# Moving steps in the hand-written order of a two-batch recurrence: second factors, outputs and weight loads

## The chip, the cores and the metric

The kernel runs on one core of a Trainium2 chip. The metric is device time in microseconds (us), median of the runs. TensorE is PE in the profile, VectorE is DVE, ScalarE is ACT, GpSimd is POOL, and SyncE (SP) only issues DMAs here.

## The reference, cut to what matters

Two layers work on x of 2 batches x 1024 tokens x 256 channels. The change touches only the first one's attention, a linear recurrence with a decay for each channel and token (4 heads of 64). Its core:

```
def step(S, inputs):
    rt, kt, vt, wt = inputs
    kv = kt[..., :, None] * vt[..., None, :]
    y = jnp.einsum('bhi,bhij->bhj', rt, S + u[None, :, :, None] * kv)
    S = wt[..., :, None] * S + kv
    return (S, y)
...
yn = ((y - mean) * jax.lax.rsqrt(var + LN_EPS)).reshape(b, t, c)
yn = yn * ln_w + ln_b
return yn @ W_o
```

Ahead of it r, k, v and w come from matrix products of the mixed input (x and its shift by one token). Behind it follow an expert stage, a sparse attention, a local attention and a feed-forward stage, all untouched by the change.

## The kernel before

`phase_b` computes the recurrence without a loop over tokens. The 1024 tokens of a batch are 8 blocks of 128. Within a block the token pairs are covered by a diagonal step and seven **levels** (h = 1, 2, 4 ... 64), each for both halves c of the channels. The steps, as they are named in the list `ORDER` (name, batch, rest):

- `m`, `x j`, `d1`, `d2`, `k`, `r`, `v`: the projections of a batch. For each `x` step, PE makes four products (L472), DVE takes them out of PSUM (L726) and adds one input (L728), and GpSimd adds three (L836).
- `D c`: the diagonal, PE at L515, DVE at L801. It reads `ru`, the second factor (r times a vector), which GpSimd makes (L842).
- `L h c`: a level. PE multiplies (L534; in batch 1 two large bf16 products of an identity, L521, whose result nobody reads, go ahead of it). Then DVE scales one factor (L738, called rE below) and for h up to 16 copies the result under a mask (L816); GpSimd scales the other factor (L853, called kF). The next level of the same half waits for both rE and kF of this one.
- `W`: block decays, seven halving products on DVE (L748). In batch 1 they write where the mixed inputs lay, so they wait until the `v` products are done.
- `kE`: PE transposes the keys (L456), ACT copies them (L676). `S c`: PE products (L551), then seven dependent state updates on DVE (L757).
- `y g`: the outputs of blocks 4g to 4g+3: PE at L571 and L575, ACT copies (L683). They wait for states of both halves. `stats`, `scale`: normalization on DVE (L768 to L785), with a square root on ACT (L687).
- `yn g`, `o g`: PE transposes (L456), ACT scales (L692), PE multiplies by W_o (L591), DVE adds to x (L826).

Every engine walks the same list and leaves out what is not its own, so the place of a step in `ORDER` sets its place on PE, DVE, ACT, GpSimd alike. `in_turn` merges lists by spreading each evenly over the whole. PSUM banks are taken in a ring of eight in the same order. The last `o` step of the phase lets the expert stage begin (PE at L1070). SyncE loads the next stage's weights (L437 to L444) over batch 0's space, behind a wait.

Of the kernel before, what the change touches and what calls it, by code (L numbers as in the profile page):

```python
# [19 lines left out]
D = 256  # L20
# [92 lines left out]
def kmaj(ap, c=2):  # L113
    return ap.rearrange("(c p) n -> p c n", c=c)
# [20 lines left out]
def adapter(K, tag, k, n_ids, idx0, names, hT, ready, ready_x):  # L135
# [6 lines left out]
    s_xb, s_var, s_std, s_norm = (K.sem(f"{tag}_{n}") for n in ("xb", "var", "std", "norm"))  # L142
    ORDER = [("z", n, b) for b in range(B) for n in range(2)] + [("y", t, 0) for t in range(TB_)] + [("y", t, 1) for t in range(4)]
    ORDER += [("T", c, g, 0) for c in range(2) for g in range(2)] + [("y", t, 1) for t in range(4, TB_)] + [("T", c, g, 1) for c in range(2) for g in range(2)]
    for s in ORDER:
        ring.plan((tag,) + s, "dve" if s[0] == "y" else "act")
# [17 lines left out]
    def pe(e, w):  # L164
        for s in ORDER:
            b, key = s[-1], (tag,) + s
            i = ring.bank(key)
            if s[0] == "z":
                n = s[1]
                w.wait_ge(s_w[b], 64)  # L170
                ready(w, b)
                w.wait_ge(*ring.free(key))
                for c in range(2):
                    h = e.matmul(PS[0:k, i, :], ws[b].wd[:, c, :], hT[b][:, c, 512 * n:512 * n + 512], start=c == 0, stop=c == 1)
            elif s[0] == "y":
                t = s[1]
                w.wait_ge(*ring.emptied((tag, "z", t // 4, b)))
                w.wait_ge(*ring.free(key))
                h = e.matmul(PS[:, i, 0:D], ws[b].zT[0:k, P * t:P * t + P], ws[b].wu[0:k, :], start=True, stop=True)
            else:  # L180
                _, c, g, _ = s
                w.wait_ge(s_norm, 8 * b + 4 * g + 4)
                w.wait_ge(*ring.free(key))
                for j in range(4):
                    h = e.transpose(PS[:, i, P * j:P * j + P], ws[b].y[:, 4 * g + j, P * c:P * c + P], K.ident)
            h.then_inc(ring.sem, 1)
# [114 lines left out]
def in_turn(*lists):  # L301

    at = [((j + 0.5) / len(z), n, s) for n, z in enumerate(lists) for j, s in enumerate(z)]
    return [s for _, _, s in sorted(at)]


def phase_b(K):
# [3 lines left out]
    a, PS, ring, X, cv, arena, ident = K.a, K.PS, K.ring, K.X, K.cv, K.arena, K.ident  # L311
# [18 lines left out]
    A, ru, kE, Wl, St, st = [], [], [], [], [], []  # L330
    for space in (arena.down(9840), shared):
# [3 lines left out]
        o, z = 6144, {}  # L335
# [23 lines left out]
    def project(b):  # L359
        return [("m", b)] + [("x", b, j) for j in range(4)] + [("d1", b), ("d2", b)] + [("W", b)] * (1 - b) + [("k", b), ("r", b), ("v", b)] + [("W", b)] * b  # L360

    def pairs(b):
        return [("D", b, c) for c in range(2)] + [("L", b, h, c) for h in LEVELS for c in range(2)]

    def close(b, late):


        norm = [("stats", b, 0), ("stats", b, 1), ("scale", b, 0), ("scale", b, 1)] if late else [("stats", b, 1), ("scale", b, 1)]
        first = [("y", b, 0)] + [("stats", b, 0)] * (1 - late) + [("y", b, 1)] + [("scale", b, 0)] * (1 - late)
        return [("kE", b), ("S", b, 0), ("S", b, 1)] + first + norm + [(n, b, g) for g in range(2) for n in ("yn", "o")]  # L370

    ORDER = project(0) + [("mx", 1)] + in_turn(pairs(0), project(1)) + in_turn(close(0, 1), pairs(1)) + close(1, 0)

    for s in ORDER:
        b = s[1]
# [29 lines left out]
    s_bx, s_decay, s_ru, s_rE, s_kF, s_W, s_S, s_var, s_sqrt, s_yn = (  # L405
        K.sem("b_" + n) for n in ("xx", "decay", "ru", "re", "kf", "w", "s", "var", "sqrt", "yn"))
# [3 lines left out]
    def n_level(b, h, c):  # L410

        return 14 * b + 2 * LEVELS.index(h) + c + 1

    def n_W(b, h):
        return 7 * b + LEVELS.index(h) + 1
# [8 lines left out]
    def lower(z, h):  # L424
        return z.rearrange("p (m two j) -> p m two j", two=2, j=h)[:, :, 0, :]
# [7 lines left out]
    K.b_done = K.end = b_done  # L433

    def sp(e, w):
        w.wait_ge(*ring.emptied(("o", 0, 3)))
        e.dma_start(K.W1c, kmaj(a["L0_cond2_W1"])).then_inc(s_wc, 16)  # L437
        for b in range(B):
            r = e.value_load(K.ids[0:1, 2 + b:3 + b], min_val=0, max_val=E - 1)
            e.dma_start(K.Wc[b][:, :, 0:192], a["L0_cond2_W2"].rearrange("(f p) n -> p f n", f=8)).then_inc(s_wc, 16)  # L440
            e.dma_start(K.Wc[b][:, :, 192:256], a["L0_cond2_We"].rearrange("e (f p) n -> e p f n", f=8)[bass.ds(r, 1)].rearrange("e p f n -> (e p) f n")).then_inc(s_wc, 16)
            e.dma_start(K.bc[b][:, 0:192], a["L0_cond2_b2"].partition_broadcast(P)).then_inc(s_wc, 16)
            e.dma_start(K.bc[b][:, 192:256], a["L0_cond2_be"][bass.ds(r, 1)].rearrange("e n -> (e n)").partition_broadcast(P)).then_inc(s_wc, 16)
        e.dma_start(K.Wg, kmaj(a["L0_ffn_Wg"])).then_inc(s_wc, 16)  # L444

    def pe(e, w):
# [147 lines left out]
        w.wait_ge(K.s_tmix_w, 128)  # L594
        for name, b, *s in ORDER:
            if name == "m":
# [231 lines left out]
    def pool(e, w, own):  # L828
        for name, b, *s in ORDER:
            if name == "x":  # L830
                j, = s
                n, c = NC[j]
                sl = slice(512 * n, 512 * n + 512)
                for f in (1, 3, 2):
                    w.wait_ge(*ring.emptied(("x", b, j, f)))
                    e.tensor_tensor(xf[f][:, c, sl], xf[f][:, c, sl], K.hT2[b][:, c, sl], ALU.add).then_inc(s_xf[f], 1)  # L836
            elif name == "D":
                c, = s
                if b:
                    w.wait_ge(*ring.filled(("v", 1, 3)))  # L840
                w.wait_ge(*ring.emptied(("r", b, 1, 1)))
                e.tensor_scalar(ru[b][:, c], rT[b][:, c], cv("faaaa", c), 1.0, ALU.mult, ALU.mult).then_inc(s_ru, 1)  # L842
            elif name == "L":
                h, c = s
                if h > 1:
                    w.wait_ge(s_W, n_W(b, h // 2))
                    w.wait_ge(s_kF, n_level(b, h // 2, c))
                else:
                    w.wait_ge(s_decay, 4 * b + 4)
                low = lower(kT[b][:, c], h)  # L850
                Wh = Wl[b][h][:, c].rearrange("p (m two) -> p m two", two=2)
                w.wait_ge(*ring.filled(("L", b, h, c, 1)))
                e.tensor_tensor(low, low, Wh[:, :, 1:2].broadcast_to([P, S // (2 * h), h]), ALU.mult).then_inc(s_kF, 1)  # L853

    return sp, pe, act, dve, pool


# [1601 lines left out]
def build(nc, a, out, stop=None):  # L2459
    with ExitStack() as ctx:  # L2460
# [20 lines left out]
        for name, phase in (("x0", phase_b), ("x1", phase_d), ("c2", phase_e), ("x2", phase_f), ("x3", phase_g)):  # L2481
            stages.append(phase(K))
            if stop == name:
                break
# [111 lines left out]
```

## Time and profile before

| | us |
|---|---|
| time, median of 3 runs | 2020.78 (2017.02 to 2028.28) |
| time of the profiled execution | 2041.56 |
| its span | 2039.8 |
| PE busy, share of the span | 1886.8, 93% |
| DVE busy | 1108.7, 54% |
| POOL busy | 459.2, 23% |
| the recurrence's merged part, from `D 0 0` on PE to its last `o` step | 102 to 334 |

The engine shares are for the whole span; the touched phase is 11% of it. There the row of the granted TensorE clock is what to look at beside the waits: it stands at full (1.00, 2.4 GHz) or half (0.50, 1.2 GHz).

### The profile page before, as it was taken

Reading aid. Unit: us, or ns where it says so; the run is one execution under the profiler, and the core shown is the slowest. Engines: PE = TensorE matmul, PEld = TensorE weight load, DVE = VectorE, ACT = ScalarE, POOL = GpSimd, SP = SyncE. Lnnn points to the kernel's source line nnn. Section 1 sums busy time; section 2 is a strip of 40 time slices with the busy share of each in tenths; the row PEclk is TensorE's granted clock in tenths of the full one; section 3 lists DMA queues with packets and bytes.
Section 4 is the critical chain, followed back from the end, with each engine's and each line's share of the span. In section 5 each row is a group of like instructions: output and inputs, shape, how many; then the busy total and the mean of one; then the engine's idle time right before and its main releaser. Section 6 shows DMA issues by size and latency. Waiting matters only on the chain.

```text
span 2039.8 us, 37916 instructions
## 1 busy us (share of the span) xinstructions
PE 1886.8 (93%) x15705; PEld 1378.7 (68%) x15705; DVE 1108.7 (54%) x2301; ACT 944.4 (46%) x1689; POOL 459.2 (23%) x512
## 2 busy tenths in 40 slices
PE   5989998995997978899999999999999999999997
PEld 3466876673664654677777777766777777787776
DVE  4474543017123125788888788854555554445544
ACT  2213022111233304788888888854455544445522
POOL 1353110004121033222121212112223222223212
PEclk8779578996998988999999999999999999999999
DMA  4000021111343347741011211000000000010001
GB/s 131 0 1 2 1 68 43 52 56 56 99 144 114 97 132 191 139 76 38 21 36 37 91 25 33 20 22 1 2 2 1 1 1 2 1 27 2 2 1 42
DMA packets 89309, 92.22 MB, mean 45 GB/s; under 512 B 34914, under 2 KB 74786, under 8 KB 88994
## 3 DMA queue, kind: packets, MB, share of 16 engines
q1 hardware_dynamic: 82882, 78.01, 14.2%
q0 software_dynamic: 3456, 9.44, 1.7%
q8 instruction: 125, 2.05, 0.4%
q10 hardware_dynamic: 2800, 2.34, 0.4%
q14 instruction: 46, 0.38, 0.1%
HBM read 67.23 MB, written 23.07 MB: 44 GB/s over the span
## 4 chain that ended last, share of the span: by engine, by line
PE 79%; ACT 7%; DVE 6%; DMA 3%; issue 2%; POOL 2%; another core or an unknown queue 0%; SPq 0%; POOLq 0%; DVEq 0%
PE PS L1627 9%; PE PS L1086 8%; PE PS L1641 7%; PE PS L1077 7%; PE PS L1952 6%; PE PS L1997 6%; PE PS L2013 5%; PE PS L1987 5%; ACT arena L1721 3%; PE PS L1618 3%; PE PS L534 3%; PE PS L1957 3%; ACT arena L1717 2%; PE PS L480 1%; PE PS L2020 1%
## 5 line engine op out<-in xcount | busy, mean ns | idle before, releaser
L1800 DVE CUSTOM_DVE_ANT_0 arena<-PS,arena 128x1024 f32<-128x1024 f32 x256 | 312.2, 1220 | 68.2 <-PE PS L1618 64.1
L1721 ACT ACTIVATE arena<-arena 128x1024 f32<-128x1024 f32 x256 | 297.4, 1162 | 9.3 <-DVE arena L1800 9.2
L1627 PE MATMUL PS<-arena 128*128 128x128 f32 x2048 | 278.4, 279 | 0.4 <-ACT arena L1717 0.2
L1627 PEld LDWEIGHTS PS<-arena 128*128 128x128 f32 x2048 | 229.2, 142 | 60.2 <-issue 27.1
L2200 POOL TENSOR_SCALAR arena<-arena 128x448 f32<-128x448 f32 (+1 forms) x256 | 153.5, 616 | 393.6 <-DVE arena L2128 392.5
L2099 ACT ACTIVATE arena<-arena 128x449 f32<-128x449 f32 (+1 forms) x256 | 161.5, 633 | 141.3 <-DVE arena L2137 141.3
L1717 ACT COPY arena<-PS 128x512 f32<-128x512 f32 x298 | 171.4, 590 | 78.3 <-PE PS L1627 77.0
L1077 PE MATMUL PS<-arena 128*128 128x512 f32 x384 | 170.2, 601 | 6.6 <-ACT arena L1183 6.6
L1086 PE MATMUL PS<-arena 128*128 128x256 f32 x768 | 172.2, 385 | 0.0
L2137 DVE CUSTOM_DVE_ANT_0 arena<-PS,arena 128x448 f32<-128x448 f32 (+1 forms) x256 | 136.8, 589 | 59.9 <-PE PS L1988 58.8
L1086 PEld LDWEIGHTS PS<-arena 128*128 128x128 f32 x768 | 147.2, 193 | 23.3 <-issue 1.8
L1618 PE MATMUL PS<-arena 96*128 96x512 bf16 x512 | 154.4, 382 | 6.4 <-DVE arena L1800 3.8
L1641 PEld LDWEIGHTS PS<-arena 128*17 128x17 f32 x4096 | 103.6, 97 | 71.3 <-issue 67.7
L1807 DVE COPY arena<-PS 128x512 f32<-128x512 f32 x214 | 147.3, 688 | 6.6 <-PE PS L1627 2.0
L1641 PE MATMUL PS<-arena 128*17 128x128 f32 x4096 | 137.8, 273 | 13.3 <-ACT arena L1730 12.8
L1240 DVE TENSOR_TENSOR arena<-PS,arena 128x512 f32<-128x512 f32 x24 | 16.6, 692 | 234.4 <-PE PS L1086 226.3
L2143 DVE COPY arena<-PS 128x512 f32<-128x512 f32 (+1 forms) x128 | 83.9, 656 | 105.4 <-PE PS L1997 104.6
L1077 PEld LDWEIGHTS PS<-arena 128*128 128x128 f32 x384 | 72.8, 192 | 96.8 <-issue 96.7
L1997 PE MATMUL PS<-arena 128*128 128x128 f32 x960 | 130.3, 277 | 1.8 <-ACT arena L2105 1.8
L1997 PEld LDWEIGHTS PS<-arena 128*128 128x128 f32 x960 | 106.4, 141 | 30.1 <-issue 25.5
L1952 PE MATMUL PS<-arena 128*128 128x512 f32 x256 | 123.2, 605 | 1.8 <-ACT arena L1739 0.8
L2013 PE MATMUL PS<-arena 128*64 128x128 f32 x1920 | 119.8, 275 | 0.0
(294 smaller groups left out, 2728.6 us busy)
## 6 DMA issues: line engine op xcount, KB each, us to landing
arena<-in_L_ffn_W SPq DMA_DIRECT2D x16, 1024.0 KB, 7.2
arena<-prior SPq DMA_DIRECT2D x16, 512.0 KB, 4.0
parts<-arena SPq DMA_DIRECT2D x24, 256.0 KB, 6.4
arena<-parts SPq DMA_DIRECT2D x96, 64.0 KB, 2.9
arena<-parts SPq DMA_DIRECT2D x48, 128.0 KB, 9.6
prior<-arena SPq DMA_DIRECT2D x4, 1024.0 KB
ye<-arena SPq DMA_DIRECT2D x7, 512.0 KB, 3.0
ya<-arena SPq DMA_DIRECT2D x7, 512.0 KB, 5.0
```

Of the source, the lines that this page charges most:

```text
L1077: h = e.matmul(PS[:, i, :], wt[:, k, P * f:P * f + P], src[:, k, s0:s0 + 512], start=k == 0, stop=k == 1)
L1086: h = e.matmul(PS[:, i, D * j:D * j + D], src[:, f, P * (t + j):P * (t + j) + P], wt[:, f, :], start=f == 0, stop=f == 7)
L1618: i = e.matmul(PS[:, SBK[z % 2] + n, :], Q6[m % 2][0:96, h, :], K6[m // TB_][0:96, h, 512 * n:512 * n + 512], start=True, stop=True)
L1627: h = e.transpose(PS[:, i, P * j:P * j + P], Sb[z % 3][:, 512 * g + P * j:512 * g + P * j + P], ident)
L1641: i = e.matmul(PS[32 * d:32 * d + 17, OBK, P * g:P * g + P], V4[b][:, k, h + d, :], Pt[(z + d) % 8][:, P * k:P * k + P], start=k == 0, sto ...
L1717: e.copy(Pt[z % 8][:, 512 * g:512 * g + 512], PS[:, group(key, r), :]).then_inc(r.into(key), 1)
L1721: e.activation(Sb[z % 3], Sb[z % 3], ACT.Exp, bias=mr[:, z % 4:z % 4 + 1], scale=-1.0).then_inc(s_exp, 1)
L1800: e.tensor_tensor_reduce(Sb[z % 3], ps, Ab[m % 2], 1.0, 3e38, ALU.add, ALU.min, mr[:, z % 4:z % 4 + 1]).then_inc(s_ttr, 1)
L1952: h = e.matmul(PS[:, i, :], wt[:, k, fs], x_[:, k, 512 * n:512 * n + 512], start=k == 0, stop=k == 1)
L1997: h = e.transpose(PS[:, 4 + d, P * j:P * j + P], Pb[x % 8][:, P * j:P * j + P], ident)
L2013: h = e.matmul(PS[c, YB, P * (t % 4):P * (t % 4) + P], wt, Pt[(2 * z + d) % 4][:, P * j:P * j + P], start=j == 0, stop=j == nj - 1)
L2099: e.activation(Pb[x % 8][:, 0:wd + 1], sbt[:, 0:wd + 1], ACT.Exp, bias=mr[:, g:g + 1], scale=-1.0, accum_out=sm[:, g:g + 1]).then_inc(s_ex ...
```

## The change

Three steps are moved and one wait is loosened.

1. `ru` of batch 1 is no longer made by GpSimd at the `D` steps but at two entries of their own, placed at the end of batch 1's projections. As that list grows from 12 to 14 entries, `in_turn` also puts every projection step of batch 1, `W 1` among them, a little earlier between the levels of batch 0.
2. Three empty entries (`("wait", 0)`, which every engine passes over) are put into batch 0's closing list, so that `y 0 0` stands behind `L 1 2 1` instead of behind `L 1 1 1`, and what follows is shifted too; `yn 0 1` and `o 0 1` leave that list and go behind `S 1 1`.
3. SyncE's weight loads wait for batch 0's second `scale` instead of its last `o`.

```diff
-    ORDER = project(0) + [("mx", 1)] + in_turn(pairs(0), project(1)) + in_turn(close(0, 1), pairs(1)) + close(1, 0)
+    c0, c1, rest = close(0, 1), close(1, 0), ("wait", 0)
+    c0 = c0[:3] + [rest, rest] + c0[3:4] + [rest] + c0[4:]
+    ORDER = project(0) + [("mx", 1)] + in_turn(pairs(0), project(1) + [("ru", 1, 0), ("ru", 1, 1)]) + in_turn(c0[:-2], pairs(1)) + c1[:3] + c0[-2:] + c1[3:]
...
-        w.wait_ge(*ring.emptied(("o", 0, 3)))
+        w.wait_ge(s_yn, 2)
...
-            elif name == "D":
+            elif name == ("ru" if b else "D"):
```

The program's lines behind it are three further down in the changed kernel. DVE at the end of batch 0's levels, before (the halving products of `W 1` are L748, rE is L738, with 8x64 for level 64 and 16x32 for level 32):

```order
89 L738 TENSOR_TENSOR arena<-arena 128x16x32 x2
90 L738 TENSOR_TENSOR arena<-arena 128x8x64
91 L748 TENSOR_TENSOR arena<-arena 128x1024
...
97 L748 TENSOR_TENSOR arena<-arena 128x16
98 L738 TENSOR_TENSOR arena<-arena 128x8x64
```

And in the changed kernel:

```order
89 L741 TENSOR_TENSOR arena<-arena 128x16x32
90 L751 TENSOR_TENSOR arena<-arena 128x1024
...
96 L751 TENSOR_TENSOR arena<-arena 128x16
97 L741 TENSOR_TENSOR arena<-arena 128x16x32
98 L741 TENSOR_TENSOR arena<-arena 128x8x64 x2
```

`W 1` now stands ahead of rE of `L 0 32 1`, which `L 0 64 1` on PE waits for; before, only rE of `L 0 64 1` stood behind it.

PE from batch 1's values (L504) to the first output (L571), before:

```order
31 L504 MATMUL PS<-arena 128x256 x16
32 L534 MATMUL PS<-arena 128x64 x32
33 L515 MATMUL PS<-arena 128x128 x16
...
43 L534 MATMUL PS<-arena 128x64 x16
44 L521 MATMUL PS<-arena 128x512 x2
45 L571 MATMUL PS<-arena 128x64 x16
```

In the changed kernel (L507 and L574):

```order
31 L507 MATMUL PS<-arena 128x256 x16
32 L537 MATMUL PS<-arena 128x64 x64
33 L518 MATMUL PS<-arena 128x128 x16
...
43 L537 MATMUL PS<-arena 128x64 x16
44 L524 MATMUL PS<-arena 128x512 x2
45 L537 MATMUL PS<-arena 128x64 x16
46 L524 MATMUL PS<-arena 128x512 x2
47 L537 MATMUL PS<-arena 128x64 x16
48 L524 MATMUL PS<-arena 128x512 x2
49 L574 MATMUL PS<-arena 128x64 x16
```

Four levels of batch 0 instead of two stand between the values and the diagonal, and two levels of batch 1 are put ahead of the first output.

## Rows read from the trace of the kernel before

**Rows 1.** Stretches of the phase: busy us of each engine, granted clock, DMA.
```profile
core 0: us, PE busy (x) PEld busy (x) DVE busy (x) ACT busy (x) POOL busy (x), PEclk, DMA share, GB/s
118.00:145.30 27.30, 24.23 (x151) 16.97 (x152) 26.26 (x31) 0.59 (x1) 22.08 (x15) 0.50 0.00 1
...
189.60:193.10 3.50, 3.50 (x33) 3.28 (x32) 3.36 (x8) 0.00 (x0) 1.01 (x1) 0.51 0.00 0
193.10:206.70 13.60, 12.18 (x179) 9.85 (x179) 11.52 (x25) 2.05 (x4) 3.00 (x2) 1.00 0.00 1
206.70:275.00 68.30, 68.30 (x447) 57.85 (x446) 38.06 (x85) 5.59 (x12) 11.83 (x9) 0.50 0.00 1
275.00:298.90 23.90, 20.38 (x229) 16.88 (x229) 8.35 (x24) 7.09 (x14) 4.67 (x3) 1.00 0.51 143
298.90:326.20 27.30, 23.10 (x122) 20.97 (x122) 11.94 (x53) 3.92 (x8) 0.00 (x0) 0.50 0.01 2
```
**Rows 2.** PE, timeline: start, us, instructions, idle before them and its releaser.
```profile
182.09 3.79 PE L534 MATMUL PS<-arena 64*128 64x64 f32 x64
189.41 3.60 PE L515 MATMUL PS<-arena 64*128 64x128 f32 x32 [3.53 <-POOL arena L842]
192.94 2.00 PE L456 MATMUL PS<-arena 128*128 128x128 f32 x16
...
206.41 6.78 PE L571 MATMUL PS<-arena 128*128 128x64 f32 x32 [1.43 <-DVE arena L757]
213.12 2.83 PE L575 MATMUL PS<-arena 64*128 64x64 f32 x24
215.88 1.03 PE L521 MATMUL PS<-arena 128*128 128x512 bf16 x2
216.84 3.68 PE L534 MATMUL PS<-arena 64*128 64x64 f32 x32
```
**Rows 3.** PE, timeline, the last levels of batch 1 and batch 0's last output.
```profile
279.51 0.59 PE L521 MATMUL PS<-arena 128*128 128x512 bf16 x2
280.04 2.00 PE L534 MATMUL PS<-arena 64*128 64x64 f32 x32
281.97 3.73 PE L591 MATMUL PS<-arena 128*128 128x256 f32 x16
```
**Rows 4.** PE, timeline, batch 1's close.
```profile
289.87 1.97 PE L456 MATMUL PS<-arena 128*128 128x128 f32 x16 [1.80 <-POOL arena L853]
...
296.57 4.95 PE L571 MATMUL PS<-arena 128*128 128x64 f32 x32 [1.73 <-DVE arena L757]
...
315.51 1.97 PE L456 MATMUL PS<-arena 128*128 128x128 f32 x8
321.67 5.93 PE L591 MATMUL PS<-arena 128*128 128x256 f32 x16 [4.20 <-ACT arena L692]
327.44 1.04 PE L456 MATMUL PS<-arena 128*128 128x128 f32 x8
329.58 3.73 PE L591 MATMUL PS<-arena 128*128 128x256 f32 x16 [1.10 <-ACT arena L692]
334.10 3.71 PE L1070 MATMUL PS<-arena 128*128 128x128 f32 x32 [0.78 <-DVE arena L826]
```
**Rows 5.** DVE, timeline: batch 0's and batch 1's halving products, levels and states.
```profile
80.74 3.43 DVE L748 TENSOR_TENSOR arena<-arena 128x1024 f32<-128x1024 f32 x7 [12.34 <-ACT arena L655]
136.18 0.77 DVE L738 TENSOR_TENSOR arena<-arena 128x512 f32<-128x512 f32 x1
136.86 1.30 DVE L816 COPY_PREDICATED arena<-arena,PS 128x512 f32<-128x512 uint8 x2
...
184.84 6.62 DVE L748 TENSOR_TENSOR arena<-arena 128x1024 f32<-128x1024 f32 x7
...
200.89 2.04 DVE L738 TENSOR_TENSOR arena<-arena 128x512 f32<-128x512 f32 x1
...
207.62 0.69 DVE L738 TENSOR_TENSOR arena<-arena 128x512 f32<-128x512 f32 x1
```
**Rows 6.** POOL, timeline.
```profile
186.06 1.76 POOL L853 TENSOR_TENSOR arena<-arena 128x512 f32<-128x512 f32 x1 [0.23 <-PE PS L534]
187.80 2.81 POOL L842 TENSOR_SCALAR arena<-arena 128x1024 f32<-128x1024 f32 x2
200.88 1.50 POOL L853 TENSOR_TENSOR arena<-arena 128x512 f32<-128x512 f32 x1 [10.26 <-PE PS L534]
```
**Rows 7.** SyncE, DMA issues: the first and the last of the ten weight loads.
```profile
286.46 0.37 SPq L437 DMA_DIRECT2D arena<-in_L_cond_W  x1
...
296.22 0.43 SPq L444 DMA_DIRECT2D arena<-in_L_ffn_Wg  x1
```

## The prediction, made before the changed kernel ran

> **What bounds the phase now.** I read the stretches with their granted clock first [rows 1], then PE's timeline and its waits [rows 2 to 4], then who released them on DVE and GpSimd [rows 5, 6]. PE is busy almost all the way from 102 to 334 us, yet for 126 of these us its clock stands at half (27.3, 3.5, 68.3 and 27.3 us) [rows 1]. So PE's own work is the bound, and its price depends on what its waits do to the clock. A level of batch 1 costs 1.03 + 3.68, start to start 4.6 us, at half clock [rows 2] and 0.59 + 2.00, start to start 2.5, at full [rows 3]. The clock fell after the wait for `ru` of 3.53 us, came back during the diagonal behind it (193.1), fell again right after the 1.43 us wait of the first output for its states, at 206.7, and then stayed low through levels and outputs for 68.3 us in which PE was never idle. Only the larger products of W_o brought it back at 275 [rows 1, 2].
>
> The change aims at both waits. I follow PE's time points through it against the profiled execution (2041.56 us, span 2039.8), whose last product of the phase lets the next stage begin at 334.1 [rows 4]. The three timed runs have a median 20.8 us lower; I carry the difference over to that median unchanged.
>
> **Step 1, the earlier projections: -2.1.** From 118 to 145 DVE is busy 26.3 of 27.3 us [rows 1] and everything there goes at its pace. In the new list `x 1 3` stands ahead of `L 0 4 0`, so DVE reaches it one level, 0.77 + 1.30 = 2.07 us, sooner [rows 5], and with it PE's `d1 1`. GpSimd could hold `L 0 4 0` back (0 gain); a level of PE work at half clock, 3.7, is the most that can be won. I take DVE's 2.1. The values end at 182.1 - 2.1 - 3.8 (two levels of batch 0, now behind them, cost 3.79 [rows 2]) = 176.2.
>
> **Step 2, the diagonal: +2.1 at its end, the gain of step 1 included.** `ru` leaves the path: its 2.81 us on GpSimd now lie between levels. But `W 1` now stands ahead of rE of `L 0 32 1`. PE: three level steps from 176.2 end at 181.9. DVE: `L 0 32 0` is ready at 178.1, then rE 0.69, `W 1` 6.62, rE 0.69 to 1.3 [rows 5]: 186.1 to 186.7. `L 0 64 1` on PE waits for this, **4.7 us instead of 3.53**. Queued behind it on PE are the diagonal, kE and all of batch 1's levels. The clock falls as it did for 3.53. `L 0 64 1` then takes 3.7 (to 190.3), the diagonal 3.6 (to 193.9) [rows 2]; the clock should be back somewhere in kE, which I charge 1.0 above its 2.0. `L 1 1 1` ends 2.1 later than before, at 206.5. So one wait of the kind is exchanged for another.
>
> GpSimd is the other half of this. `W` of batch 0 took 3.43 us, that of batch 1 6.62 while GpSimd ran kF and `ru` beside it [rows 5, 6]; rE took 2.04 when kF had begun 0.01 us ahead of it and 0.69 otherwise [rows 5, 6]. In the new order GpSimd again has four or five operations within `W 1`. So I take 6.62, with 3.43 as the other bound.
>
> The Trainium skill (SBUF — State Buffer, on the shared port pair) says that a VectorE operation with two SBUF inputs and a GpSimd operation that reads SBUF lock each other out rather than share. By that rule `W 1` stays long in its new place; without it the wait would be 1.5 us. The 2.04 beside 0.69 speaks for the rule.
>
> **Step 3, the output moved behind two levels: +0.8 of waiting, and no cover.** Before, the output waited 1.43 for the states. Now `L 1 2 0` (2.5 us) fills that gap, but the next level, `L 1 2 1`, waits for rE of `L 1 1 1`, which DVE does behind the states of `S 0 1`. That ended at 208.3 [rows 5]; it is 2.1 later, and kF of `L 1 2 0` now starts just ahead of it, so 0.7 to 1.4 more as in the 2.04 case: 211.3. PE is ready at 206.5 + 2.6 = 209.1, waits 2.2, and the clock falls, as it did for 1.43.
>
> From 206.4 to the end of `L 1 64 1` at 288.0 PE had 81.6 us of work without a gap. From 211.3 the same work lacks `L 1 2 0` (-4.6) and `yn 0 1` with `o 0 1` (1.1 + 3.7, -4.8 [rows 3]). But `o 0 0`, which brought the clock back, stands one step later: two levels more go at half clock (+4.2). 211.3 + 76.4 = **287.7, against 288.0**: nothing gained.
>
> **Step 4, batch 0's last output as cover: +3.9, -7.4.** The wait for kF of `L 1 64 1` (1.80) and kE, `S 1 0`, `S 1 1` stay. `yn 0 1` and `o 0 1` come behind them: 1.0 + a wait for ACT as at 329.58 (1.1) + 3.7 [rows 4] + 0.6 of L521, and `y 1 0` no longer waits 1.73. It starts at 300.5 instead of 296.57, +3.9. Then the clock: before, it fell at 298.9 during that output, and both outputs took 18.9 us (296.57 to 315.5) [rows 1, 4]. With the longer W_o products right ahead and no wait on states, I expect it full: all at half they would be 21.2, so about 11.5 at full by the ratio 3.68 to 2.00 of a level [rows 2, 3]. End 312.0, **-3.5 against 315.5**. If it stays as before the end is 320, +5. The tail (17.8 us to 333.3, with its waits for normalization, 4.20 and 1.10 [rows 4]) hangs on the end of `y 1 1` through stats, square root and scale, and I leave it as it is.
>
> **Step 5, weight loads: 0.** The ten issues at 286.5 to 296.2 [rows 7] move to the end of the second `scale`, some 10 us or more ahead, where DMA is idle (0.00) [rows 1]. Their data is used in the next stage, after 334; no queue is moved past. Nothing to gain, nothing to lose.
>
> **Sum:** -3.5 us: 2041.56 becomes 2038.1, the median 2020.8 becomes 2017.3.
>
> **Rivals.**
> *Cover holds (A).* If the clock does not fall at 211, ten levels save 2.1 each and two outputs about 4.5 each: -30. But DVE then has about 40 us of levels, states, normalization in the stretch against PE's 43, so PE would soon wait on it; I take -20: 1997. For it: between 275 and 289 levels ran at full clock, past a 1.80 us wait. Against: 1.43 was enough to lose it, and mine is 2.2.
> *`W 1` is short (B).* With 3.43 the wait is 1.5 us, 3.2 less, and `L 0 64 1`, the diagonal and kE stay at full: another -4.2. Then 2010. Against it: GpSimd is as busy as before.
> *The last part stays at half clock (C).* Step 4 gives +5.5 instead of -3.5: 2026. For it: the falls at 206.7 and 298.9 came behind waits of only 1.43 and 1.73 us, and the 1.80 us wait at kE is still there.
> *Slower (D).* The 4.7 us wait takes the clock down, and the kE and diagonal products don't bring it back: the short level products of batch 1 never did in 68.3 us. Then kE, `D 1 1`, both `S` and three levels cost 11 more, less 2.2 for the wait at 211 that disappears: +9. It decides from the point where the clock is still at half when kE ends; with C it is 2035, alone 2026. Against: before, the diagonal's first 3.6 us were enough.
>
> The Trainium skill (TensorE: Matmul & The Clock Gate, on the HAM clock gate) calls half clock the default, released by activity, and watched on a schedule of its own that does not start with the kernel. By that rule runs of the same kernel may keep or lose the clock at the same wait, which is why A, C and D are rivals and not mishaps. That the three timed runs spread over 11 us and the profiled one lies 21 above their median agrees.
>
> **Chances.** Forecast 0.57 (2017, itself 2010 to 2024), A 0.13, B 0.10, C 0.12, D 0.08. The limit of 0.5% (about what a measurement of this kernel can tell from no change) is 10 us. Faster: A, half of B, and the forecast's edge, 0.23. Slower: most of D, a little of C, 0.08. Within: 0.69. Range 2001 to 2030: it leaves out the better part of A and the worse of D and C.
>
> **What would show it.** Right: `L 0 64 1` released by DVE L741 after 4 to 5 us; no PE wait on `ru`; `L 1 2 1` released by L741 after about 2 us; half clock from about 211 to 282; `y 1 0` and `y 1 1` in some 11.5 us; the next stage beginning near 330. Wrong: `W 1` near 3.4, or full clock past 215, or half clock past 200 without a return.

## The result, and the profile after

The changed kernel takes 2030.44 us (median of 7 runs, 2026.51 to 2033.76) against 2020.78 before (7 runs, 2017.02 to 2028.28): ratio 1.0047, 95% interval 1.0028 to 1.0065. It is about 10 us slower. Yet its profiled execution took 2029.75 us, 11.8 us less than the profiled one of before. This contradiction is the subject of what follows.

PE's timeline after, with the places that answer to [rows 2 to 4] (start, us, instruction, idle before it and its releaser):

```profile
178.45 5.85 PE L537 MATMUL PS<-arena 64*128 64x64 f32 x96
189.22 3.68 PE L537 MATMUL PS<-arena 64*128 64x64 f32 x32 [4.91 <-DVE arena L741]
...
211.60 0.97 PE L524 MATMUL PS<-arena 128*128 128x512 bf16 x2 [2.10 <-DVE arena L741]
...
286.76 3.62 PE L459 MATMUL PS<-arena 128*128 128x128 f32 x16 [1.80 <-POOL arena L856]
...
294.98 3.73 PE L594 MATMUL PS<-arena 128*128 128x256 f32 x16 [1.10 <-ACT arena L695]
298.99 3.68 PE L574 MATMUL PS<-arena 128*128 128x64 f32 x32
...
328.75 3.71 PE L1073 MATMUL PS<-arena 128*128 128x128 f32 x32 [0.78 <-DVE arena L829]
```

The wait for `ru` is gone and `L 0 64 1` waits 4.91 us for rE (L741) instead; `L 1 2 1` waits 2.10 us; the first output of batch 1 follows its L524 products without a wait, and its matmuls run at full clock (3.68 us where [rows 4] had 4.95). The granted clock of three stretches of the changed kernel (columns as in [rows 1]):

```profile
195.00:211.00 16.00, 14.49 (x220) 11.95 (x216) 13.99 (x30) 2.54 (x6) 4.29 (x3) 1.00 0.00 1
212.00:276.00 64.00, 64.00 (x437) 54.57 (x436) 36.36 (x79) 5.31 (x14) 12.82 (x9) 0.50 0.00 1
...
293.00:310.00 17.00, 15.90 (x148) 14.64 (x146) 8.73 (x40) 2.74 (x5) 0.00 (x0) 1.00 0.00 1
```

It falls at the 2.10 us wait, stands at half for 64 us without an idle moment of PE, and is full in the two outputs of batch 1. Two shorter falls belong to other waits: from about 188 to 195 us, begun in the wait of 4.91, and from about 287 to 290, behind the 1.80 for kF. DVE and GpSimd after (first DVE's `W 1`, rE of `L 1 1 0` and rE of `L 1 1 1`, then GpSimd's kF of `L 1 1 0`):

```profile
181.21 7.35 DVE L751 TENSOR_TENSOR arena<-arena 128x1024 f32<-128x1024 f32 x7
...
203.46 2.04 DVE L741 TENSOR_TENSOR arena<-arena 128x512 f32<-128x512 f32 x1
...
210.18 1.36 DVE L741 TENSOR_TENSOR arena<-arena 128x512 f32<-128x512 f32 x1
```

```profile
203.45 1.50 POOL L856 TENSOR_TENSOR arena<-arena 128x512 f32<-128x512 f32 x1 [8.81 <-PE PS L537]
```

A useful yardstick is the **phase**, from the first `D` product on PE to the first product of the expert stage (L1070, L1073 after). In the two profiles it is 102.37 to 334.10, 231.7 us, before, and 103.64 to 328.75, 225.1 us, after. The prediction said 3.5 us less against that profile; it is 6.6 less.

### The profile page after: what moved, and what is told of

Same layout as the page of the kernel before. It is cut to its first block, busy times and chain, and to the rows that moved or that the text cites. A ratio compares the mean times of both kernels' runs of the same rounds, so it can differ in the third digit from the quotient of the medians.

```text
span 2027.9 us, 37915 instructions
## 1 busy us (share of the span) xinstructions
PE 1880.9 (93%) x15705; PEld 1372.7 (68%) x15705; DVE 1111.5 (55%) x2301; ACT 944.9 (47%) x1689; POOL 460.6 (23%) x512
## 4 chain that ended last, share of the span: by engine, by line
PE 80%; ACT 7%; DVE 6%; DMA 3%; issue 2%; POOL 1%; SPq 0%; POOLq 0%; DVEq 0%
PE PS L1630 9%; PE PS L1089 8%; PE PS L1080 7%; PE PS L1644 7%; PE PS L1955 6%; PE PS L2000 6%; PE PS L2016 6%; PE PS L1990 5%; ACT arena L1724 3%; PE PS L1621 3%; PE PS L1960 3%; PE PS L537 3%; ACT arena L1720 2%; PE PS L483 2%; PE PS L2023 1%
## 5 line engine op out<-in xcount | busy, mean ns | idle before, releaser
L1243 DVE TENSOR_TENSOR arena<-PS,arena 128x512 f32<-128x512 f32 x24 | 16.6, 692 | 227.9 <-PE PS L1089 227.9
```

## The experiments

Two questions were open: is the profiled execution of before typical, and if not, what decides? A time with its ratio is against runs of the kernel before taken beside it on the same chip. Phases are from the profile of each. Outside the phase the profiled executions took between 1798.9 us (e8) and 1811.9 us (e3), so a phase explains a time only to within some us.

### e1: the kernel before again

> The kernel before, unchanged, for a second profile and the span and clock of each timed run. Theory K (the profile of before was not a typical execution): in most runs its clock holds past the 1.43 us wait of the first output, so that this phase ends some 10 to 15 us sooner than the 334 us of the first profile; the profiled execution then lies near 2020 us with a mean clock above 0.937, and its stretch 207 to 230 us stands at full clock. Theory L (the loss of the change lies behind this phase): the new profile again shows half clock from 207 to 275 and the next stage beginning at 333 to 335, and the 20 us between profile and timed runs lie in later stages. The clocks and spans of the timed runs decide as well: under K they cluster at 2016 to 2026 us with 0.945 or more and now and then one at 2040 with 0.937.

Measured: 2024.99 us (five runs at 2019.1 to 2022.2, five at 2027.8 to 2031.5), ratio 0.9999 (0.9976 to 1.0022), profiled execution 2020.22 us, phase 97.98 to 313.07 = 215.1 us, **16.6 us shorter than in the first profile of the same kernel** (the two executions differ by 21.3 us, so 4.7 lie elsewhere). PE around the first output:

```profile
199.51 0.61 PE L521 MATMUL PS<-arena 128*128 128x512 bf16 x2
200.22 3.76 PE L571 MATMUL PS<-arena 128*128 128x64 f32 x32
...
226.63 1.03 PE L521 MATMUL PS<-arena 128*128 128x512 bf16 x2 [2.83 <-DVE arena L738]
```

The granted clock behind it (columns as in [rows 1]):

```profile
207.00:228.00 21.00, 18.17 (x226) 14.94 (x226) 15.57 (x35) 1.29 (x3) 7.03 (x5) 0.97 0.01 2
228.00:253.00 25.00, 22.61 (x151) 18.71 (x150) 19.73 (x43) 3.23 (x7) 4.32 (x4) 0.50 0.00 1
```

PE has no wait of as much as 0.2 us for the states, and the clock stays full until the 2.83 us wait that ends at 226.6. There it falls too, but it is back at about 254: some 27 us of half clock in place of the 68.3 of [rows 1]. "Keeps the clock" means below that it holds through the first output, not that it holds to the end.

Over all 88 timed runs of this kernel in the study 71 lie at 2025.5 us or less, 16 at 2027 to 2033.4 and one at 2042.7. The profiled execution that the prediction was made from, at 2041.56, belongs to the rare ones. The share differs by chip: 24 of 40 runs lie in the lower group on the chip of e1 to e4, 41 of 41 on the chips of e5 to e11, 6 of 7 on that of the result. The groups are told by time. The mean granted clock of a run, where it is recorded, is 0.945 to 0.953 in the lower group and 0.935 to 0.948 in the upper one, so a run near the border can't be assigned. Theory K holds in its outcome, with another reason than it gave (in this profile there was no wait to hold past), and L falls.

GpSimd and DVE at `L 1 1 0` in e1, to be compared with [rows 5, 6] and with the rows after:

```profile
196.01 2.07 POOL L853 TENSOR_TENSOR arena<-arena 128x512 f32<-128x512 f32 x1 [11.29 <-PE PS L534]
```

```profile
196.02 0.69 DVE L738 TENSOR_TENSOR arena<-arena 128x512 f32<-128x512 f32 x1
...
201.43 0.69 DVE L738 TENSOR_TENSOR arena<-arena 128x512 f32<-128x512 f32 x1
```

In all traces in which nothing orders them the two operations begin within 10 to 20 ns of each other. GpSimd's is released by the products of `L 1 1 0`. DVE comes free at that very moment, its last state update of `S 0 0` ending about 0.04 us before rE starts. Here GpSimd's was held up (2.07 us) and DVE's took 0.69; in the first profile and in the changed kernel it is the other way (1.50 and 2.04). The loser pays some 0.6 to 1.4 us. Only DVE's loss matters, since the states of `S 0 1` stand behind it.

### e2 and e3: the parts alone

e2 keeps the earlier `ru` and leaves the outputs and the loads as before:

```diff
+    ORDER = project(0) + [("mx", 1)] + in_turn(pairs(0), project(1) + [("ru", 1, 0), ("ru", 1, 1)]) + in_turn(close(0, 1), pairs(1)) + close(1, 0)
...
+            elif name == ("ru" if b else "D"):
```

> Only batch 1's second factors made earlier, with the two further entries in the projections' list (W 1 comes ahead of L 0 32 1 as in the changed kernel); outputs and weight loads as before. Theory K: the PE wait of about 4.9 us before L 0 64 1 takes the clock down for about 10 us, and the first output stands behind L 1 1 1 as before with its wait of 1.4 us; whether the clock holds there is as in the kernel before: time 2018 to 2026 if it holds, 2030 or more if it falls. Theory L: no change of the loss in this part, 2020. The wait on ru (3.53 us at the diagonal) is gone in either.

Measured: 2032.08 us (2022.28 to 2035.41, 10 runs), ratio 1.0030 (1.0001 to 1.0058), phase 221.0 us. DVE loses the tie (rE 2.04 at 203.22), the first output waits 1.41 us, the clock falls. So this part alone has a loss, its interval just clear of 1. The wait of 4.91 us behind `W 1` is there as in the changed kernel; e11 takes it away.

e3 moves the outputs only:

```diff
+    c0 = c0[:3] + [rest, rest] + c0[3:4] + [rest] + c0[4:]
+    ORDER = project(0) + [("mx", 1)] + in_turn(pairs(0), project(1)) + in_turn(c0[:-2], pairs(1)) + c1[:3] + c0[-2:] + c1[3:]
```

> Only the outputs of batch 0 moved (three empty entries, last output among batch 1's); second factors, W 1 and weight loads as before. Theory K: the 2.1 us wait of L 1 2 1 for rE of L 1 1 1 takes the clock down near 210 in every run, where the kernel before mostly keeps it: 2026 to 2032, and the phase ends 5 to 10 us later than in a run of before that keeps the clock. Theory L: this part only shortens the phase (the last output covers a wait), 2012 to 2018, and what the change loses is lost by W 1 or later.

Measured: 2013.46 us (2004.79 to 2027.98), ratio 0.9964 (0.9931 to 0.9997), phase 200.8 us. I had expected 2026 to 2032, and that was wrong: in the profile `L 1 2 1` did not wait for as much as 0.2 us, because DVE won the tie:

```profile
204.45 2.07 POOL L855 TENSOR_TENSOR arena<-arena 128x512 f32<-128x512 f32 x1 [11.31 <-PE PS L536]
```

```profile
204.46 0.69 DVE L740 TENSOR_TENSOR arena<-arena 128x512 f32<-128x512 f32 x1
...
209.87 0.69 DVE L740 TENSOR_TENSOR arena<-arena 128x512 f32<-128x512 f32 x1
```

The ten runs fall into two groups, six at 2005 to 2014 and four at 2026 to 2028 (mean granted clock 0.952 to 0.958 and 0.943 to 0.947). This made me form theory M: **the tie decides whether PE waits, and the wait whether the clock is lost for 60 us**.

### e4: the output between the two levels

```diff
+    ORDER.remove(("y", 0, 0))
+    ORDER.insert(ORDER.index(("L", 1, 2, 1)), ("y", 0, 0))
```

> The changed kernel with one step moved: y 0 0 stands between L 1 2 0 and L 1 2 1 instead of behind L 1 2 1. L 1 2 0 then covers the wait for the states and y 0 0 covers rE of L 1 1 1, so PE has no wait of over 1 us from the diagonal to the second output. Theory K: the clock holds past 211 at least until 225, and the phase ends 5 to 15 us sooner than the 328.8 us of the changed kernel: 2015 to 2025 us. Theory L: the middle makes no difference for the loss, 2028 to 2032.

Measured: 2014.55 us (2005.35 to 2016.30, 9 runs), ratio 0.9949 (0.9932 to 0.9966), phase 202.0 us. DVE lost the tie in the profile (rE 2.04 at 197.72) and it did no harm: `y 0 0` followed `L 1 2 0` with no wait, and the clock held to the wait at 234.7. All nine runs lie within 11 us. One step's place is worth some 20 us by the ratios to the kernel before, 0.9949 against 1.0047 (16 by the two times, which are from different chips).

### e5, e6 and e7: the tie forced

e5 (kernel before) and e7 (changed kernel) let DVE go first:

```diff
                 w.wait_ge(*ring.filled(("L", b, h, c, 1)))
+                if (b, h, c) == (1, 1, 0):
+                    w.wait_ge(s_rE, n_level(1, 1, 0))
                 e.tensor_tensor(low, low, Wh[:, :, 1:2].broadcast_to([P, S // (2 * h), h]), ALU.mult).then_inc(s_kF, 1)
```

e6 (kernel before) has DVE wait on `s_kF` in the same manner.

> The kernel before with one added wait: GpSimd's kF of L 1 1 0 waits for DVE's rE of L 1 1 0, which it meets in the same 10 ns in every trace so far. Theory M (this tie decides the clock): rE now always takes 0.69 us and never 2.04, the first output does not wait for its states, the clock holds past 207 in nearly every run, and the runs lie at 2016 to 2025 us with clocks of 0.947 or more; the group at 2027 to 2043 thins out from about one run in three to one in ten. Theory N (the clock's own schedule decides, whoever wins the tie): the two groups stay as they are, median 2022 to 2025.

> The opposite forced on the kernel before: DVE's rE of L 1 1 0 waits for GpSimd's kF, so it starts 1.5 us later in every run, as when GpSimd wins the tie. Theory M: the first output waits 1.4 us in every run, half clock from about 207 to 270, runs at 2027 to 2043 us with clocks of 0.947 or less, median near 2031. Theory N: two groups as before, median 2022 to 2026 (at most 1.4 us later for the wait itself).

> The changed kernel with the same added wait as e5 (GpSimd's kF of L 1 1 0 behind DVE's rE). Theory M: rE of L 1 1 0 takes 0.69, rE of L 1 1 1 ends 1.4 to 2 us sooner, L 1 2 1 waits under 0.7 us instead of 2.1, the clock holds past 211 to about 235, and the time falls from 2030 to 2005 to 2016. Theory N: the 4.9 us wait before L 0 64 1 is what costs, and the time stays at 2027 to 2032.

| | time, us | all runs, us | ratio | phase, us |
|---|---|---|---|---|
| e5, before, DVE first | 2017.27 | 2015.7 to 2022.2 | 0.9997 (0.9985 to 1.0009) | 215.2 |
| e6, before, GpSimd first | 2027.12 | four at 2019.4 to 2022.8, six at 2027.0 to 2036.0 | 1.0040 (1.0019 to 1.0060) | 228.6 |
| e7, changed, DVE first | 2010.11 | 2005.9 to 2010.5 | 0.9950 (0.9931 to 0.9969) | 204.7 |

An added wait on GpSimd makes the changed kernel 20 us faster, in all four runs. In e7 PE has no wait from 189.7 to 241, where the changed kernel waited 2.10 at 211.6 and lost the clock until 276. (In e7 it falls at about 243, behind the 2.17 us, and is back at about 263.)

```profile
189.65 3.68 PE L537 MATMUL PS<-arena 64*128 64x64 f32 x32 [4.91 <-DVE arena L741]
...
241.09 0.60 PE L524 MATMUL PS<-arena 128*128 128x512 bf16 x2 [2.17 <-DVE arena L741]
```

```profile
196.00:240.00 44.00, 42.81 (x572) 36.30 (x570) 34.76 (x71) 4.20 (x8) 13.12 (x10) 1.00 0.01 1
```

On e5's chip the runs of before all lay at 2014.6 to 2023.9, the good group, which is why e5 could gain nothing there; e6 is the telling one. There the first output waits 1.67 us and PE's clock falls:

```profile
208.74 7.01 PE L571 MATMUL PS<-arena 128*128 128x64 f32 x32 [1.67 <-DVE arena L759]
```

```profile
210.00:269.00 59.00, 58.99 (x399) 49.77 (x399) 34.03 (x79) 3.90 (x8) 10.76 (x8) 0.50 0.00 1
```

But in four of ten runs it came out at 2019 to 2023, with a mean granted clock of 0.947 to 0.949 (the other six 0.937 to 0.945). So M was too strong. The tie decides the wait; whether a wait of this size loses the clock seems to differ from one execution to the next. That is read from times and mean clocks, for no run of the four was profiled.

### e10: the wait kept, the idleness taken away

```diff
         def level(b, h, c):
+            if (b, h, c) == (1, 2, 1):
+                k = group(("L", b, h, c, 0))
+                for _ in range(8):
+                    dense(k)
```

> The changed kernel with eight more of the bf16 products whose result nobody reads (8 x 0.27 us) in front of the wait of L 1 2 1: PE is busy during the wait, and nothing comes earlier. If it is the clock that costs (theory M and K): no fall near 211 although L 1 2 1 still starts when rE of L 1 1 1 is done, the phase ends about 15 to 20 us sooner, time 2008 to 2016. If it is the waits themselves, or DVE's later rE, that cost the 10 us: no gain, 2029 to 2033.

Measured: 2008.90 us (2003.13 to 2014.28, 7 runs), ratio 0.9961 (0.9945 to 0.9978), phase 208.0 us against 225.1. DVE lost the tie here too, and `L 1 2 1` did not start any sooner after `L 1 2 0` (212.2 less 208.07, against 211.6 less 207.49 in the changed kernel):

```profile
208.07 2.00 PE L541 MATMUL PS<-arena 64*128 64x64 f32 x32
210.00 1.90 PE L524 MATMUL PS<-arena 128*128 128x512 bf16 x8
212.18 0.60 PE L524 MATMUL PS<-arena 128*128 128x512 bf16 x2 [0.28 <-DVE arena L745]
```

```profile
200.00:244.00 44.00, 41.54 (x538) 33.76 (x537) 36.12 (x71) 2.37 (x5) 13.34 (x10) 1.00 0.01 1
```

1.90 us of products that nobody reads save 21 us against the changed kernel beside it (e9). It is what happens to the clock that costs, not the lateness of rE. Taken alone e10 doesn't tell whether the idle moment or the missing products matter to the clock; e4 and e7, which take the idle moment away without a product more, keep it too.

### e9, e11 and e8: the changed kernel again, and W 1 early

e11 is the changed kernel with `W 1` behind the keys. The space of its results is exchanged with that of `ru` and `kE`, so that it overwrites the mixed input of k instead of that of v:

```diff
-        return [("m", b)] + [("x", b, j) for j in range(4)] + [("d1", b), ("d2", b)] + [("W", b)] * (1 - b) + [("k", b), ("r", b), ("v", b)] + [("W", b)] * b
+        return [("m", b)] + [("x", b, j) for j in range(4)] + [("d1", b), ("d2", b)] + [("W", b)] * (1 - b) + [("k", b)] + [("W", b)] * b + [("r", b), ("v", b)]
...
-                w.wait_ge(*ring.filled(("v", 1, 3)))
+                w.wait_ge(*ring.filled(("k", 1, 1, 1)))
```

e8 adds e4's place for `y 0 0` and e7's wait to it.

> The changed kernel, unchanged, beside e10 and e11 on their chip. Theory M: DVE's rE and GpSimd's kF of L 1 1 0 start within 10 to 20 ns of each other, GpSimd wins, rE takes 2.04 us, L 1 2 1 waits 2.1 us, the clock falls: 2026 to 2034 us in all or nearly all runs, some 10 us above the runs of before. If the tie goes the other way on this chip, rE takes 0.69, and the runs lie at 2006 to 2012.

> The changed kernel with W 1 right behind the keys alone (its space exchanged with that of ru and kE), without the moved output and without the added wait of e8. It prices the 4.9 us wait before L 0 64 1. Theory M: that wait and the half clock behind it go (about 7 to 9 us), but what happens at the tie of L 1 1 0 still decides the stretch from 211 on: about 2020 to 2024 if GpSimd wins, 2002 to 2006 if DVE wins. Rival: the whole loss of the changed kernel is the 4.9 us wait, and this version lies at 2008 to 2014 whoever wins.

> A version to beat both: the changed kernel with W 1 right behind the keys (its space exchanged with that of ru and kE, so that it overwrites the mixed input of k and not that of v), y 0 0 between L 1 2 0 and L 1 2 1, and e7's added wait. Theory M and the step account: no wait of PE between batch 1's values and the diagonal (before 3.53, changed kernel 4.91), so no half clock near 190; that is 4.9 us of wait and about 4 of half clock less than e4: 2003 to 2008 us. If the wait before L 0 64 1 is covered by something else that is late (the masked copies behind W 1, or PSUM banks), a wait of 2 to 4 us shows in its place and the time is 2008 to 2014.

e9: 2029.99 us, eight runs at 2026.1 to 2032.9 and two at 2004.2 and 2010.1; ratio 1.0041 (1.0006 to 1.0076). The result repeats on another chip. The two shorter runs of ten have a mean granted clock of 0.957, the others 0.941 to 0.944, so they seem to be this program with its clock kept.

e11: 2023.97 us, eight runs at 2021.3 to 2028.5, two at 1999.9 and 2004.8; ratio 1.0012 (0.9975 to 1.0048), phase 222.0 us. The 4.91 us wait is gone (1.21 at kE instead), and the wait of 2.10 at `L 1 2 1` still loses the clock. The early `W 1` is worth 6 us against e9 by the medians, 4 by the larger groups, 3 by the phase: less than the 7 to 9 that M expected. In the profile the wait of 2.10 us comes 6 us sooner after the phase's start, but the clock is then low for some 74 us instead of 64. Five of the eight longer runs lie above the 2020 to 2024 that M gave. The rival, that the whole loss was the long wait, falls: it asked for 2008 to 2014 whoever wins the tie.

e8: **2001.97 us** (1993.06 to 2004.44, 4 runs), ratio 0.9920 (0.9901 to 0.9939), phase 194.2 us, faster than both kernels and just below the 2003 to 2008 expected. Its one wait of PE between batch 1's values and the diagonal's end, and the first one in the levels of batch 1:

```profile
181.89 1.97 PE L462 MATMUL PS<-arena 128*128 128x128 f32 x16 [1.21 <-POOL arena L861]
226.82 1.03 PE L527 MATMUL PS<-arena 128*128 128x512 bf16 x2 [2.17 <-DVE arena L744]
```

## Why the prediction was wrong

**What bounds the phase** was right: PE's time there is set by what waits do to its clock.

**Step 1** was too large. From the first `D` to the end of the values the kernel before took 79.7 us [rows 2], the changed one 74.8; of the 4.9, 3.8 are the two levels moved behind. It gained 1.1, not 2.1.

**Step 2** held: 4.91 us of wait against 4.7 (`W 1` took 7.35 beside GpSimd, not 6.62). `L 1 1 1` ended 1.3 us later after the phase's start than before, against 2.1 forecast.

**Step 3** held in its waits, 2.10 against 2.2, and the clock fell. Its work was overcharged: 73.4 us to the end of `L 1 64 1` instead of 76.4, since the clock came back at about 276.5, right behind `yn 0 0` and before `L 1 64 0`. The prediction had only the larger products of W_o bring it back; here it was back before they began (L594 at 278.9).

**Step 4** held: `y 1 0` without a wait, both outputs in 11.1 us (11.5 forecast) at full clock. Two figures of Step 4 don't add up as written: its terms put the start of `y 1 0` at 300.9, not 300.5, and 300.5 + 18.9 is 319.4, so the half-clock case (rival C) is +3.9, not +5 or +5.5. Neither bears on the outcome. **Step 5** held: the loads were issued from 276.9 to 288.4, and PE waited for none of them in the phase.

**The sum** was therefore right against the profiled execution in sign, and short in size (-3.5, measured -6.6 in the phase). The step that failed is the one from the trace to the median, the sentence "I carry the difference over to that median unchanged". The trace described an execution that had lost its clock at the first output, and most runs of that kernel do not. Like with like, by the phase: both lost, 231.7 to 225.1, -6.6; both kept, 215.2 (e5) to 204.7 (e7), -10.5. But by their times the kernel before kept the clock in 71 of 88 runs, and the changed kernel lost it in 15 of 17. Kept to lost is 215.2 to 225.1, +9.9, and the measured difference is +9.7. That the two agree to 0.2 us is luck, as the rest of an execution varies by more.

No rival had this. A asked whether the changed kernel would keep its clock; that the kernel before already did, so that the change could lose it, was the case to put on the other side. A itself was sound: where e7 keeps the clock the phase is 27.0 us shorter than in the first profile, against the 23.5 that A comes to (-3.5 and -20), and PE does wait on DVE soon after, 2.17 us at 241. The clue was in front of me: the profiled execution stood 20.8 us above the median of its own kernel, and I named it as a spread of the clock without asking which stretch of the trace was then untypical. The 2.04 us of rE [rows 5], with kF 0.01 us ahead of it [rows 6], was read as a fixed cost, and is a tie that goes either way.

The Trainium skill (SBUF — State Buffer, on the shared port pair) says that whichever of the two operations issues first holds the pair and the other blocks. The traces bear it out, with a reservation: in e1 and e3 GpSimd's row starts 0.01 us ahead and is still the one held up, so 10 ns of a timeline don't tell the winner. The durations do. As an estimate from the rows, an operation held up for the whole of the other would end 0.69 + 1.50 = 2.19 us after both began; it ended after 2.04 (DVE) and 2.07 (GpSimd).

**What stays open:** why GpSimd wins the tie once `ru` is made early. In all six traces with the early `ru` and a free tie (the changed kernel, e2, e4, e9, e10, e11) rE took 2.03 or 2.04 us; of the three with `ru` at the `D` steps (the first profile, e1, e3) it did in one. The 4.91 us wait is not the reason: e11 has the early `ru` without that wait, and GpSimd won the tie in its trace and eight of its ten runs took 2021 us or more. The starts lie 10 to 20 ns apart in either case, and no run varied alone what comes just before the tie. Open too is what lets some executions keep the clock through the same wait (e6).

## What to carry to other kernels

Before a prediction is made from one trace, hold its time against the timed runs: if it lies apart, find the stretch that may differ, and cost the change from both sides of it. Where PE runs short products, look for short idle moments (the falls that cost most here stood behind waits of 1.4 to 2.9 us) and either order the steps so that another engine's latency is covered (e4, e8) or fill them with products that nobody reads (e10). Where operations of two engines begin at the same moment and one holds the other up, don't count on either winning. An explicit wait that lets the critical one go first cost nothing that could be measured in e5 (ratio 0.9997) and put the four runs of e7 within 5 us.

## What the runs showed of the hardware

- In the changed kernel's profile the half clock (1.2 GHz, granted 0.50) stood for 64.00 us in which PE was never idle. Most of the same steps ran at the full clock (1.00) for 44 us in e7 and e10. In the former PE had been idle for 2.10 us just before, in the latter it had not (e7 no wait, e10 0.28 us).
- The same wait need not lose the clock. The 1.80 us wait for the last kF passed at full clock in the first profile and in e1, and was followed by about 3 us of half clock in the changed kernel.
- A DVE operation with two SBUF inputs and a GpSimd operation beginning within 20 ns: 0.69 and 2.07 us when DVE wins (e1, e3), 2.04 and 1.50 when GpSimd wins (first profile, changed kernel, e2, e4).
- Seven halving products on DVE took 3.43 us alone [rows 5], 6.62 (first profile) and 7.35 us (changed kernel) beside a busy GpSimd, and 4.95 in e8 and e11, where `W 1` stands earlier.
